# Graph convolution over an 8192 x 8192 adjacency on one core: dividing the far pieces of the adjacency between the two load queues by rows instead of by columns

## The reference

```python
h = maximum(layernorm(x), 0)
A_hat = adj + eye(8192)                      # A_hat from adj and the identity
d_inv_sqrt = sum(A_hat, axis=1) ** -0.5      # needs every element of each row
out = (d_inv_sqrt[:, None] * A_hat * d_inv_sqrt[None, :]) @ (h @ W.T)
return x + relu(out)
```

## Time and profile before

| | us |
|---|---|
| timed executions | 1187.28, 1238.79, 1252.42 |
| their median | 1238.79 |
| the profiled execution's own time | 1192.53 |
| its span, first to last instruction | 1190.7 |
| PE / DVE / ACT / POOL busy in it | 979.3 / 813.2 / 578.5 / 128.7 |
| moved by DMA | 381.32 MB, mean 320 GB/s |

### The profile page before, as it was taken

One profiled execution on the slowest core, in us unless ns is written; L12 is line 12 of the kernel. 1 busy time (PEld: TensorE's weight loads), 2 busy tenths in 40 slices (PEclk: granted clock), 3 DMA queues, 4 the chain that ended last, 5 costly groups with the idle time before them and its releaser, 6 DMA issues.

```text
span 1190.7 us, 9309 instructions
## 1 busy us (share of the span) xinstructions
PE 979.3 (82%) x2363; PEld 448.5 (38%) x2363; DVE 813.2 (68%) x969; ACT 578.5 (49%) x1719; POOL 128.7 (11%) x102
## 2 busy tenths in 40 slices
PE   0634356668489797989979999999999899899997
PEld 0631122223234243434434444444444344344443
DVE  5442244456467576767868788888888788687785
ACT  2898685776565646362635625215436552110011
POOL 3121021020110101010000101001001000010011
PEclk9876667789789898989989999999999999999999
DMA  9899999999999999999999999999999959999994
GB/s 297 309 360 383 390 397 362 367 384 349 357 362 335 361 333 341 329 336 304 328 281 363 277 338 329 336 300 296 319 305 267 324 156 284 290 266 316 330 331 116
DMA packets 266628, 381.32 MB, mean 320 GB/s; under 512 B 10448, under 2 KB 246096, under 8 KB 266576
## 3 DMA queue, kind: packets, MB, share of 16 engines
q1 hardware_dynamic: 133360, 190.40, 51.2%
q10 hardware_dynamic: 133216, 190.34, 51.0%
HBM read 376.50 MB, written 4.19 MB: 320 GB/s over the span
## 4 chain that ended last, share of the span: by engine, by line
PE 43%; DMA 3%; ACT 2%; DVE 2%; ACTq 1%; issue 1%; POOLq 0%; SPq 0%; DVEq 0%
PE bank L502 42%; DMA slot<-in_adj_dram 3%; ACT junk L550 2%; DVE adjT L698 1%; DVE part L682 1%; ACTq L286 1%; PE pre L478 0%; ACT slot L540 0%; ACTq L294 0%; DVE kept_cell L783 0%; ACT kept_cell L568 0%; POOLq L187 0%; PE sums_bank L466 0%; ACTq L328 0%; SPq L286 0%
## 5 line engine op out<-in xcount | busy, mean ns | idle before, releaser
L502 PE MATMUL bank<-adjT,support 128*128 128x512 f32 x2048 | 934.2, 617 | 115.7 <-DVE adjT L698 110.6
L698 DVE STREAM_TRANSPOSE adjT<-slot 128x1024 f32<-128x1024 f32 x430 | 521.6, 1232 | 206.2 <-PE bank L502 102.0
L502 PEld LDWEIGHTS bank<-adjT,support 128*128 128x128 f32 x2048 | 401.3, 198 | 626.7 <-issue 622.8
L550 ACT ACTIVATE junk<-slot 128x384 bf16<-128x384 f32 (+2 forms) x732 | 348.1, 477 | 255.3 <-issue 197.0
L540 ACT ACTIVATE slot<-slot 128x6144 f32<-128x6144 f32 (+11 forms) x56 | 166.4, 2971 | 159.5 <-issue 85.0
L550 ACT ACTIVATION_READ_ACCUMULATOR junk<-slot 128x1 f32 x732 | 136.6, 187 | 0.0
L422 POOL COPY kept_cell<-slot 128x2048 f32<-128x2048 f32 x35 | 65.1, 1892 | 593.4 <-DMA slot<-in_adj_dram 475.3
L568 ACT ACTIVATE kept_cell<-kept_cell,dinv 128x128 f32<-128x128 f32 x64 | 20.2, 389 | 173.1 <-DVE kept_cell L792 68.4
L698 DVE STREAM_TRANSPOSE adjT<-kept_cell 128x1024 f32<-128x1024 f32 x70 | 85.6, 1235 | 26.5 <-PE bank L502 26.5
L682 DVE TENSOR_REDUCE part<-slot 128x4 f32<-128x1536 f32 (+2 forms) x61 | 94.3, 1561 | 8.9 <-DMA slot<-in_adj_dram 8.9
L466 PE MATMUL sums_bank<-by_block,spread 128*128 128x64 f32 x32 | 7.5, 326 | 45.6 <-DVE by_block L733 45.6
(11 more groups left out here) (53 smaller groups left out, 181.3 us busy)
## 6 DMA issues: line engine op xcount, KB each, us to landing
slot<-in_adj_dram ACTq DMA_DIRECT2D x134, 768.0 KB, 13.6
slot<-in_adj_dram SPq DMA_DIRECT2D x134, 768.0 KB, 15.4
slot<-in_adj_dram ACTq DMA_DIRECT2D x66, 512.0 KB, 12.7
slot<-in_adj_dram SPq DMA_DIRECT2D x66, 512.0 KB, 13.7
slot<-in_adj_dram ACTq DMA_DIRECT2D x8, 1536.0 KB, 15.7
slot<-in_adj_dram SPq DMA_DIRECT2D x8, 1536.0 KB, 16.0
slot<-in_adj_dram ACTq DMA_DIRECT2D x4, 1408.0 KB, 17.0
slot<-in_adj_dram SPq DMA_DIRECT2D x4, 1408.0 KB, 17.9
```

Of the source, the lines that this page charges most:

```text
L502: ins = nc.tensor.matmul(bank[bank_of(g)][:], support[:, v * R + t, :], adjT[at % TURNS][:, r, :], start=(n == first_of[g] and t == 0), st ...
L550: nc.scalar.activation(junk[at % JUNKS][:, :n], cells[:, c, :], ACT.Copy, accum_out=part[u % 2][:, k, c:c + 1]).then_inc(junk_done, 1)
L698: nc.vector.transpose(adjT[at % TURNS][:].rearrange("p t (c i) -> p t c i", i=Q), half.rearrange("p c (t r) -> p t c r", r=Q)).then_inc(t_ ...
```

## The change

`load_far` divides a band between the queues by rows. SP's DMA brings rows 0 to 63 of the band with all four column quarters into partitions 0 to 63, and ACT's rows 64 to 127 into partitions 64 to 127. Before, each brought all 128 rows with two quarters. The number of DMAs, the bytes of each (half of the band), the length of the contiguous runs and their number for each DMA (128 x 2 before, 64 x 4 after) stay the same, as does what lies where in the slot once both have landed.

```diff
         def load_far(queue, quarters, m):
             kind, u, bb, n, v, cells = landing[m]
             to = far_block(m).rearrange("p a (b j) -> p a b j", b=B)
-            b0 = quarters[0]
+            p = slice(quarters[0] * Q, (quarters[-1] + 1) * Q)
             for a in range(n):
-                queue.dma_start(to[:, a, b0:b0 + 2, :],
-                                adj_far[u, :, bb + a, b0:b0 + 2, v * CELL:(v + cells) * CELL]
+                queue.dma_start(to[p, a, :, :],
+                                adj_far[u, p, bb + a, :, v * CELL:(v + cells) * CELL]
                                 ).then_inc(ld_slot[slot_of[m]], 16)
```

## The result

The changed kernel took 1234.03 us in the median of four executions (1226.14 to 1253.16), the kernel before 1245.61 (1187.28 to 1255.49, four executions too). When only the executions near each kernel's own fastest are compared, the ratio is 1.0322, 95% interval 1.0163 to 1.0481. The kernel before scatters by 6% here, so ratio and medians point in different directions. Over all its executions in this study (51, from 1186.32 to 1275.44 us) its median is 1238.6 us, and that of the changed kernel (10, from 1226.14 to 1253.16) is 1236.7. A good part of this study is about what lies behind that. The profiled execution took 1226.14 us, its span is 1224.3 us.

The account below looks back on a forecast made before the run. Landing DMA pieces were taken to bound the kernel until about 600 us, PE afterwards. Terms 4.6 + 1 - 6 = -0.4 us meant no change; the middle of four known executions gave 1216 us, range 1187 to 1285, likeliest 1190 to 1245.

Parts of the forecast that it names:

- What bounds the kernel: Up to about 600 us the rate at which DMA pieces land bounds the kernel; after that PE does.
- Issue: Far DMA issues on ACT (463 ns) and SP (369 ns) were taken as unchanged; 11 us more on ACT would be hidden.
- Far bytes under both queues: Far pieces loaded by both queues, each writing one half of the partitions: 2% of 232 us, +4.6 us.
- rival A: Long far packets of both queues collide in one half: +50 us, 1266 us, if a third go so; chance 0.30.
- Queues that run alone: Early stretches with one queue nearly alone on far pieces fall to 232 GB/s; a gap hides the tail; +1 us.
- Going over: Thirteen switches between far and cell pieces up to 482 us lose 18.9 us; a third is recovered, -6 us.
- The kernel's own variation: Unchanged kernel varies by over 5%; the forecast took the middle of four known executions, 1187.28 to 1252.42 us.
- rival C: Going over between far and cell pieces costs nothing any more: -13 us, 1203 us; chance 0.18.
- Rival B: Both queues' far pieces together get only one queue's 232 GB/s: +179 us, 1395 us; chance 0.04.

## Why the prediction was wrong

The forecast was no change, 1216 us, likeliest range 1190 to 1245; the measured ratio was 1.0322. The measured median, 1234.03 us, lies inside that range, and the medians are level. That is luck: of the two effects that meet here, the loss was forecast at less than a tenth of its size, and the bad executions of the kernel before, against which the change gains, were not in the sum.

- What bounds the kernel: right. By 600 us the changed kernel had moved 12.6 MB less, 36 us at 350 GB/s; the seam moved by 35.5 us and the span by 33.6.
- Issue: the size was off, the conclusion nearly right. ACT's issue went from 463 to 572 ns and SP's from 369 to 550. That was almost hidden, as 140 issues in place of 56 showed; in the chain of waits ACT's far issues make up 7.9 us instead of 3.4.
- "Far bytes under both queues, +4.6 us": this is the step that failed. I worked out what halves cost with 1536-byte runs (1.4%) and carried it over to runs of 6144 bytes. There the cost is 31%, at 3584 bytes it is 18% (332 against the 404 that the kernel before made there), at 2048 bytes 7% (359 against 387). In bytes: by 360 us the changed kernel had moved 17.5 MB less, some 50 us at 350 GB/s. With the measured rates, each run length against its own rate before, the far pieces of 4 to 12 cells take some 67 us more, an estimate. That is the mis-sized term: 67 where +4.6 stood. It is rival A, priced at 50 us; A was given 0.30. Its rate of 250 GB/s was too low and its share of a third of the bytes too small: all the wide pieces were slower, at 286 to 332 GB/s.
- Queues that run alone: the drop was right (231 GB/s where 365 stood, 232 expected), the gap that should have hidden it was not there. SP's eighth far issue ends at 53.4 us instead of 45.6 and its next issue starts at 64.04 instead of 57.01; the engines' share in the first 60 us went from 0.93 to 1.03. The start is thus 7.0 us later, where I had taken 1 us. How much of it comes from lone queues and how much from the slower rate under both was not separated.

```profile
10.73 42.63 SPq L294 DMA_DIRECT2D slot<-in_adj_dram  x8
...
64.04 1.32 SPq L286 DMA_DIRECT2D slot<-in_adj_dram  x2
```

- Going over, -6 us: the direction was right and the size too small. From 360 to 600 us the changed kernel moved 4.9 MB more than the execution I had the trace of (14 us at 350 GB/s), and 16.5 MB more than the same kernel run again. I counted 18.9 us of losses in a lucky execution. Part of what I counted was hardly a mix of both kinds: from 476 to 482 us 816 of 918 packets were those of cell pieces, both queues were at work, and the rate was 241 GB/s.
- The kernel's own variation: I saw 5% between executions and looked at one trace. The slower execution differs from it almost only behind 360 us, in the stages of these goings-over. That the medians of the two kernels are level comes from this second effect, which I had only as rival C.
- Rival B: not so. Two queues on disjoint halves moved 355 GB/s together with 1536-byte runs and 286 with 6144, against 231 and 217 when one was nearly alone. By the Trainium skill (SBUF — State Buffer, "Can I just issue two DMAs to hit both halves?") the second transfer adds only 6%; these numbers give 24% and more, and a gain that depends on the length of the runs, of which the section says nothing. The Trainium skill (SBUF — State Buffer, Door 1: The DMA port swizzle) also says that a transfer to one half reaches half of the ports. The trace roughly agrees: 231 GB/s from a nearly lone queue on one half, 405 from one on all 128 partitions.

## What to carry to other kernels

When two load queues each write their own half of the partitions, measure the rate at the run length you will use: here it fell from 359 GB/s at 2048 bytes to 286 at 6144, while transfers over all 128 partitions rose from 387 to 417. When a stage mixes whole-width and half-width DMAs, look in short stretches of the trace at the rate and at the share of each queue, not only at the sum of the shares: the engines were busy all the time at 369 GB/s, at 241 and at 208. And before you believe 3%, run the unchanged kernel against itself.

## What the runs showed of the hardware

- The rate of half-width far DMAs falls with the run length (359, 340, 350, 332, 325, 317, 314, 306, 286 GB/s from 2048 to 6144 bytes). The side that is written causes it (293 against 418 GB/s). That the packets of both queues meet in one half was argued from the rates and not shown.
- Queues can fall into taking turns and out of it again for long: in the run of the kernel before that took 1238.6 us they did so from 492 us to beyond 550, at 208 to 222 GB/s in five stretches where one was nearly alone. In the traces of kernels that had runs of at most 1536 bytes in the far pieces of up to 7 cells, or half-width DMAs there, one queue was nearly alone for no more than 8 of the 240 us from 360 to 600; the two kernels without a fixed half for each queue are among them, with one execution each. In those of the other kernels it was 3 to 46 us.
- A DMA with four rows of runs for each of 64 partitions took ACT 572 ns to issue and SP 550, one with two runs for each of 128 partitions 463 and 369, though both have 256 runs. Where only the source was changed it was 576 and 562, where only the destination was, 639 and 618.
